# GpSimd holds back its work on the last pair until VectorE's joint chain of moments is through

## The reference

```python
for i in range(4):
    q, k, v = x @ Wq[i] + bq[i], x @ Wk[i] + bk[i], x @ Wv[i] + bv[i]
    Q, K = elu(q) + 1, elu(k) + 1
    KV, Ksum = sum over tokens of K * v, sum over tokens of K
    V = Q * KV / (Q * Ksum + 1e-6)
    x = ln(gelu(gelu(V @ Wo[i] + bo[i])) + x, ln1_s[i], ln1_b[i])
    x = ln(gelu(gelu(x @ W1[i] + b1[i]) @ W2[i] + b2[i]) + x, ln2_s[i], ln2_b[i])
x = layernorm(x_in + x)
h = layernorm(gelu(x @ ternary(W_fc).T), ln_w, ln_b)
x = layernorm(x + h @ ternary(W_proj).T)
```

## Time and profile before

| | |
|---|---|
| median of 3 runs | 479.62 us (478.72 to 481.2) |
| the profiled execution | 478.65 us, span 476.5 us |
| PE busy | 442.0 us (93%) |
| DVE busy | 402.6 us (85%) |
| ACT busy | 371.9 us (78%) |
| POOL busy | 13.9 us (3%) |
| DMA | 10.40 MB, mean 22 GB/s |

### The profile page before, as it was taken

The page is one execution under the profiler, slowest core; times in us unless marked ns, Lnnn a source line. Parts: engine busy times, 40 slices in busy tenths (PEclk is TensorE's granted clock), DMA queues, the critical chain, the costliest instruction groups (busy, mean ns, idle before and its releaser), DMA issues.

```text
span 476.5 us, 6527 instructions
## 1 busy us (share of the span) xinstructions
PE 442.0 (93%) x2074; PEld 309.2 (65%) x2074; DVE 402.6 (85%) x1391; ACT 371.9 (78%) x483; POOL 13.9 (3%) x19
## 2 busy tenths in 40 slices
PE   7697999999999999999999999999989999799992
PEld 6465665756575656566656665667566756688992
DVE  5988889995989698969896988698878897978897
ACT  3989877989897989798889888989888717778106
POOL 0000000000000000000000000000000003230000
PEclk9978999999999999999999999999999999999997
DMA  8200000000100000001000000000010102000003
GB/s 285 70 2 0 22 3 0 1 0 1 45 0 2 23 0 1 1 0 45 0 2 1 1 0 1 0 1 2 0 45 12 34 7 82 2 0 23 2 23 132
DMA packets 5360, 10.40 MB, mean 22 GB/s; under 512 B 848, under 2 KB 1872, under 8 KB 5328
## 3 DMA queue, kind: packets, MB, share of 16 engines
q1 hardware_dynamic: 5040, 9.47, 6.1%
q10 hardware_dynamic: 288, 0.52, 0.3%
HBM read 7.90 MB, written 2.10 MB: 21 GB/s over the span
## 4 chain that ended last, share of the span: by engine, by line
PE 41%; DVE 32%; ACT 19%; issue 7%; DMA 1%; ACTq 0%; SPq 0%; DVEq 0%
PE tile L1249 10%; PE tile L1268 7%; PE tile L1226 6%; PE tile L1222 6%; PE tile L1223 5%; DVE stats L770 5%; ACT y L369 3%; DVE y L911 3%; DVE nt L777 2%; ACT y L374 2%; PE tile L1339 2%; PE tile L1328 2%; ACT aa L388 2%; DVE y L880 2%; ACT kq L348 2%
## 5 line engine op out<-in xcount | busy, mean ns | idle before, releaser
L1249 PE MATMUL tile<-h,w 128*128 128x512 f32 x256 | 113.9, 595 | 0.9 <-ACT h L395 0.7
L1222 PE MATMUL tile<-xh,wh 128*128 128x512 f32 x224 | 97.6, 436 | 6.1 <-DVE xh L793 3.4
L1223 PE MATMUL tile<-xh,wl 128*128 128x512 f32 x224 | 89.2, 398 | 0.0
L1249 PEld LDWEIGHTS tile<-h,w 128*128 128x128 f32 x256 | 47.4, 190 | 54.8 <-issue 51.7
L395 ACT ACTIVATE h<-tile,vec 128x1024 f32<-128x1024 f32 x64 | 71.0, 1117 | 13.1 <-PE tile L1226 12.3
L1226 PE MATMUL tile<-xl,wh 128*128 128x512 f32 x224 | 71.1, 398 | 0.7 <-DVE xl L298 0.3
L403 ACT ACTIVATE nt<-tile,work 128x128 f32<-128x128 f32 x140 | 50.7, 482 | 11.3 <-DVE work L739 11.3
L1222 PEld LDWEIGHTS tile<-xh,wh 128*128 128x128 f32 x224 | 42.6, 190 | 24.9 <-DVE xh L793 5.3
L770 DVE BATCH_NORM_STATS2 stats<-tile 128x6 f32<-128x128 f32 x256 | 52.8, 280 | 0.1
L1226 PEld LDWEIGHTS tile<-xl,wh 128*128 128x128 f32 x224 | 41.6, 188 | 13.5 <-DVE xl L799 2.7
L1223 PEld LDWEIGHTS tile<-xh,wl 128*128 128x128 f32 x224 | 42.8, 191 | 9.1 <-issue 2.2
(11 more groups left out here) (173 smaller groups left out, 669.6 us busy)
## 6 DMA issues: line engine op xcount, KB each, us to landing
x<-x_t SPq DMA_DIRECT2D x7, 512.0 KB, 4.1
out_r<-x SPq DMA_DIRECT2D x8, 256.0 KB, 2.0
raw_u<-layers SPq DMA_DIRECT2D x4, 256.0 KB, 3.2
w<-layers SPq DMA_DIRECT2D x4, 256.0 KB, 3.3
raw_a<-layers SPq DMA_DIRECT2D x4, 192.0 KB, 2.8
x<-x_t ACTq DMA_DIRECT2D x2, 256.0 KB, 3.9
wo<-layers SPq DMA_DIRECT2D x4, 64.0 KB, 4.2
fc<-fc_t SPq DMA_DIRECT2D x1, 256.0 KB, 6.5
```

Of the source, the lines that this page charges most:

```text
L1222: pe.matmul(dst, wh[:, w0:w0 + P], xh[:, part(n, p, at)], start=True, stop=False)
L1223: pe.matmul(dst, wl[:, w0:w0 + P], xh[:, part(n, p, at)], start=False, stop=False)
L1249: mm = pe.matmul(dst, w2[:, (t - 1) // 2 % 2, j * P:(j + 1) * P], h[:, p, j * PAIR + at:j * PAIR + at + BANK], start=(j == 0), stop=(j == ...
```

## The change

It does three things. GpSimd gets two waits ahead of `shifted(pool, 3)`, on both halves of the tail's joint chain. `moments` and `rsqrt_of` are written anew as one helper to each level, and `moments` calls them level by level. The wait with which `moments` ended for the "g" norm (of the hidden layer) has moved into `final_sum`, which waits on `moment["g"]` or `moment["x"]` itself; six of its first instructions so carry one semaphore more. Wrappers with new names (`first_input`, `vectors`, `input_high`, `warm_up` and the like) hold the same calls in the same order.

```diff
@@ gpsimd
             shifted(pool, 1)
             with_constant(pool, 1)
             shifted(pool, 2)
+            for q in range(2):
+                pool.wait_ge(moment["2"][q], MOMENT_STEPS * STEPS)
             shifted(pool, 3)
             with_constant(pool, 0)
             with_constant(pool, 2)
@@ vector
-            def moments(*norms):
...
-                rsqrt_of([(w[0], w[1] + 2, w[2], float(width_of[n[0]]) ** 0.5) for n, w in work_of.items()])
-                for n in norms:
-                    done, base, (rstd, shift, m, v, a, b) = work_of[n]
-                    dve.wait_ge(done, base + 9)
-                    if n[0] != "g":
-                        dve.scalar_tensor_tensor(shift, m, -0.5, rstd, ALU.mult, ALU.mult).then_inc(done, 1)
+            def guess_squared(k, t, p):
+                done, base, (rstd, shift, m, v, a, b), width = chain(k, t, p)
+                dve.wait_ge(done, base + 3)
+                dve.tensor_tensor(a, b, b, ALU.mult).then_inc(done, 1)
...
+            def row_shift(k, t, p):
+                done, base, (rstd, shift, m, v, a, b), width = chain(k, t, p)
+                if k != "g":
+                    dve.wait_ge(done, base + 9)
+                    dve.scalar_tensor_tensor(shift, m, -0.5, rstd, ALU.mult, ALU.mult).then_inc(done, 1)
 
             def moments(*norms):
+                for level in (sums, mean_square, variance, guess, guess_squared, near_one, quadratics, first_product, root,
+                              row_shift):
+                    for n in norms:
+                        level(*n)
...
             def final_sum(p, u):
                 n, q = p // 2, p % 2
                 dve.wait_ge(x_cb[p], 1)
+                if n == 0:
+                    dve.wait_ge(moment["g"][q], HIDDEN_STEPS)
+                else:
+                    dve.wait_ge(moment["x"][q], 3 * MOMENT_STEPS)
                 for z in range(HALF):
```

More of the change, by code:

```diff
@@ L674, in _, with chain @@
         def _(dve):
-            def norm_work(k, t, p, u=None):
-                pair, rows = home(k, t, p), slice(0, ROWS) if u is None else slice(u * HALF, (u + 1) * HALF)
+            def chain(k, t, p):
+                pair = home(k, t, p)
                 if k == "h":
[L680 to L683, removed]
@@ L741, in rsqrt_of @@
[L741 to L764, removed]
@@ new lines, in chain, with sums @@
+                    done, first, at = moment["x"][p], 2 * MOMENT_STEPS, "g"
+                else:
+                    done, first, at = moment[k][p], call_of(k, t) * (HIDDEN_STEPS if k == "g" else MOMENT_STEPS), k
+                return done, first + 3, [value(at, pair, z) for z in range(NCOLS)], {"g": 1, "h": FF}.get(k, P)
+            def sums(k, t, p):
+                done, base, (rstd, shift, m, v, a, b), width = chain(k, t, p)
+                at = home(k, t, p)
+                if k == "g":
+                    for u in range(2):
+                        means = tile[TAIL_SLOTS["p", at, u]][:, :].rearrange("p (b c) -> p b c", c=BANK)[:, :, P:2 * PW:PW]
+                        dve.wait_ge(p_mm[p], 2 * t + u + 1)
+                        dve.tensor_copy(m[:, u * HALF:(u + 1) * HALF].rearrange("p (b c) -> p b c", c=2), means).then_inc(
+                            done, 1)
+                    dve.wait_ge(squared[at], FT)
+                    dve.tensor_scalar(b, squares[:, at, :], 1.0 / FF, OUTER_EPS, ALU.mult, ALU.add).then_inc(done, 1)
+                    return
+                if k == "h":
+                    dve.wait_ge(squared[at], FT)
+                    even, odd, even2, odd2 = (stats_h[:, p, :, c] for c in (1, 4, 2, 5))
+                else:
+                    dve.wait_ge(stats_ready[k][p], call_of(k, t) + 1)
+                    even, odd, even2, odd2 = (stats[k][:, at, :, c] for c in (1, 4, 2, 5))
+                dve.tensor_tensor(a, even, odd, ALU.subtract).then_inc(done, 1)
+                dve.tensor_tensor(b, even2, odd2, ALU.add).then_inc(done, 1)
+                dve.tensor_tensor(m, even, odd, ALU.add).then_inc(done, 1)
@@ new lines, in mean_square, with variance @@
+            def mean_square(k, t, p):
+                done, base, (rstd, shift, m, v, a, b), width = chain(k, t, p)
+                if k == "g":
+                    dve.wait_ge(done, base)
+                    dve.scalar_tensor_tensor(a, m, -1.0, m, ALU.mult, ALU.mult).then_inc(done, 1)
+                else:
+                    dve.wait_ge(done, base - 2)
+                    dve.scalar_tensor_tensor(a, a, width / 4.0, a, ALU.mult, ALU.mult).then_inc(done, 1)
+            def variance(k, t, p):
+                done, base, (rstd, shift, m, v, a, b), width = chain(k, t, p)
+                dve.wait_ge(done, base + 1)
+                if k == "g":
+                    dve.tensor_tensor(v, a, b, ALU.add).then_inc(done, 1)
+                else:
+                    dve.scalar_tensor_tensor(v, b, width * (BLOCK_EPS if k in "12" else OUTER_EPS), a, ALU.add,
+                                             ALU.add).then_inc(done, 1)
@@ new lines, in guess @@
+            def guess(k, t, p):
+                done, base, (rstd, shift, m, v, a, b), width = chain(k, t, p)
+                dve.wait_ge(done, base + 2)
+                dve.tensor_scalar(b.bitcast(I32), v.bitcast(I32), -0.5, GUESS, ALU.mult, ALU.add).then_inc(done, 1)
+            def guess_squared(k, t, p):
+                done, base, (rstd, shift, m, v, a, b), width = chain(k, t, p)
+                dve.wait_ge(done, base + 3)
+                dve.tensor_tensor(a, b, b, ALU.mult).then_inc(done, 1)
@@ new lines, in near_one, with quadratics @@
+            def near_one(k, t, p):
+                done, base, (rstd, shift, m, v, a, b), width = chain(k, t, p)
+                dve.wait_ge(done, base + 4)
+                dve.scalar_tensor_tensor(a, a, (LEAD * width ** 0.5) ** 0.25, v, ALU.mult, ALU.mult).then_inc(done, 1)
+            def quadratics(k, t, p):
+                done, base, (rstd, shift, m, v, a, b), width = chain(k, t, p)
+                lead = (LEAD * width ** 0.5) ** 0.25
+                dve.wait_ge(done, base + 5)
+                dve.scalar_tensor_tensor(v, a, Q1 * lead, a, ALU.add, ALU.mult).then_inc(done, 1)
+                dve.scalar_tensor_tensor(shift, a, Q2 * lead, a, ALU.add, ALU.mult).then_inc(done, 1)
@@ new lines, in first_product, with root @@
+            def first_product(k, t, p):
+                done, base, (rstd, shift, m, v, a, b), width = chain(k, t, p)
+                dve.wait_ge(done, base + 6)
+                dve.scalar_tensor_tensor(b, v, C1 * (LEAD * width ** 0.5) ** 0.5, b, ALU.add, ALU.mult).then_inc(done, 1)
+            def root(k, t, p):
+                done, base, (rstd, shift, m, v, a, b), width = chain(k, t, p)
+                dve.wait_ge(done, base + 8)
+                dve.scalar_tensor_tensor(rstd, shift, C2 * (LEAD * width ** 0.5) ** 0.5, b, ALU.add, ALU.mult).then_inc(done, 1)
@@ L1344, in projected, with warm_up @@
                     mm.then_inc(p_mm[p % 2], 1)
-            pe.wait_ge(const_ready, 7)
-            for _ in range(WARM_UP):
-                pe.matmul(tile[3][:, 0:P], ones[:, :], ones[:, :], start=True, stop=True)
+            def warm_up():
+                pe.wait_ge(const_ready, 7)
+                for _ in range(WARM_UP):
+                    pe.matmul(tile[3][:, 0:P], ones[:, :], ones[:, :], start=True, stop=True)
+            warm_up()
             attention_in("k", 0, 0)
```

78 lines of the change are left out of this document (23 added, 55 removed).

## The result

The changed kernel takes 475.28 us in the median of 6 executions (474.29 to 476.38), the kernel before 479.09 in the median of 6 (478.58 to 481.2). The ratio is 0.9918, with a 95% interval from 0.9904 to 0.9933. The profiled execution takes 475.41 us with a span of 473.5, 3.0 us less than the span before. Its time fell by 3.24 us, from 478.65: 0.24 us of that lies outside the span, in what an execution takes beyond its first to last instruction.

What follows compares the result with a forecast made beforehand. No engine bounds throughout; the last chain changes hands, and GpSimd stalls VectorE's joint chain by 3.01 us. Of this 2.63 arrives, other edits cost 0: 479.62 - 2.6 = 477.0 us, range 475.9 to 479.3.

Steps and rivals of the forecast that it cites:

- The stall and its size: Joint chain on VectorE: two levels, L751 and L754, stand while GpSimd works, 0.83 and 2.18 too long, 3.01 us together.
- How much arrives: From the joint chain to the outer norm's statistics: 2.63 of the 3.01 us arrives and stays whole to the end.
- Both receivers that I let decide: At pair 3's rows: TensorE's matmuls until 407.80 and ScalarE's `hidden_gelu` until 406.56 limit how much earlier work can start.
- The short wait of TensorE for ScalarE's rows: At pair 3's rows: a TensorE idle time of 0.1 replaces the present one.
- No stall elsewhere: VectorE's twelve rows of L777, read from PSUM beside GpSimd's shift and constant, still take 3.9 us; upper bound 3.5 us.
- the rival that moves the stall there: The stall moves to `rows`, eleven of which stand until 409.15: 0.2 to 0.3 us slower, 479.9; chance 0.05.
- their cover: GpSimd's last two constants end 1.0 us before the hidden layer's chain needs both inputs in SBUF; that margin stays.
- The waits of `final_sum`: Six first instructions of the last sums wait for one semaphore more: taken as 0, upper bound 0.4 us.
- the edits that were priced at nothing: Helpers and wrappers leave the instruction order on VectorE, ScalarE, TensorE and SyncE unchanged and cost nothing; `final_sum` waits taken as 0.
- the sum: Whole kernel: profiled 478.65 - 2.63 = 476.0; the same difference on the median, 479.62 - 2.6 = 477.0, 0.54% less.
- theory A: From the experiments: time at 1.2 GHz near the start has nothing to do with the edit; ratio back to 0.993 to 0.9945.
- D: Theory from the experiments: the edit changes how long TensorE runs at 1.2 GHz near the start; ratio 0.991 to 0.992.

Runs made afterwards that it cites:

- The waits alone: Kernel before plus only the two GpSimd waits ahead of pair 3's shift: 476.23 us against 478.89, ratio 0.9928; again 475.59 against 479.17, ratio 0.9926.
- the helpers alone: Changed kernel without the two GpSimd waits (helpers, wrappers, moved waits stay): 478.94 us against 478.89, ratio 0.9998; again 479.2, ratio 1.0001.
- the kernel with two memsets: Changed kernel plus two 128x2560 GpSimd memsets in a row from the landing of pair 3's input: 478.25 us in a single execution.
- the longer hold: Kernel before plus a third GpSimd instruction, a 128x1024 sum between pair 3's shift and pair 0's constant: 481.39 us against 479.17, ratio 1.0045.

## Why the prediction was right, and where it was wrong

- **The stall and its size: right.** Each level beside GpSimd takes 0.25 once it is alone; the joint chain ends at 405.1 with 3.0 less in it. The waits alone take the stall away, the helpers alone leave it.
- **How much arrives: right.** 2.63 was worked out, 2.70 measured between the two marks. Both receivers that I let decide, ScalarE in its `hidden_gelu` and TensorE in its last matmuls, are where they were put, and the statistics wait for TensorE (0.45 us) and not for VectorE's own list, as worked out. The short wait of TensorE for ScalarE's rows (0.1) did not come.
- **No stall elsewhere: right.** Twelve rows took 3.92 beside a shift and a constant; the rival that moves the stall there falls. The constants ended at 424.66, 1.04 us ahead of the first instruction of the hidden layer's chain with both inputs in SBUF, so their cover stayed.
- **The waits of `final_sum`: mis-sized.** Taken as 0, they measured 0.1 us in the traces: 61.61 to 61.65 us behind the second mark in four profiles of the change, 61.42 to 61.56 in seven of the kernel before, 61.45 and 61.57 with the waits on GpSimd alone, and 61.60 and 61.65 with the helpers and moved waits alone. (A span is given to 0.1 us, so each has 0.05 of play.) The chain that ended last shows where, at the first sum of pair 1, which in the kernel before begins right behind the hidden layer's chain. Before, and then the change:

```profile
455.10 0.18 DVE work_g L764
455.28 0.02 issue
455.30 2.16 DVE y L949 x8
```
```profile
452.00 0.18 DVE work_g L765
452.18 0.03 issue
452.21 0.02 DVEq L957
452.23 0.06 issue
452.29 0.16 DVE y L966
452.45 0.10 issue
452.55 1.89 DVE y L966 x7
```

The eight sums end 2.18 us behind the chain before and 2.26 behind it in the change. On the other side, the edits that were priced at nothing also take 0.23 us off what lies outside the span, which the prediction did not consider. Its reading of the earlier trace rows, that a fulfilled wait shows nothing, did not carry over to this place.
- **The step that failed is the sum**: "The same difference on the median gives 479.62 - 2.6 = 477.0." It took the difference within one profiled execution for that of all, and so put at nothing, without a reason, whatever the stall costs in the executions that were not profiled. Measured were 479.09 and 475.28, 3.8 us apart. Of the 1.7 us between the forecast of 477.0 and 475.28, 0.5 is the base, a median of three executions that six put lower, and 1.2 is the difference. I had seen TensorE's 2.16 us of idle time and had priced it at its length alone. In part of the executions the kernel before pays for it a second time, 1.28 us through the lower clock, and no profile of the change shows that part. By the executions at 0.981 or less, the kernel before loses 479.00 - 478.65 = 0.35 us in the mean by it. It is a rough estimate: the mean clock does not tell a loss at 410 us from one more at the start (the kernel with two memsets read 0.981 with 13.7 us at the start and none at 410; the second profile of the helpers alone read 0.983 with 6.8 and 3.4), so the share may be larger or smaller. This term explains a part of the miss and not all of it.
- **What like with like gives.** TensorE runs at 1.2 GHz for 3.4, 6.8, 10.2 or 13.7 us in all between 21 and 46 us, in any kernel. Profiles with 10.2 and no loss behind the stall: 478.51 us in the mean of five of before, 475.68 of three of the change, 2.83 apart. The stretch (2.7), the waits of `final_sum` (-0.15) and the time outside the span (0.24) add up to 2.8. So between comparable executions nothing is missing.
- **What stays open.** All 24 executions of the change have a mean of 475.38, the 89 of before 479.00 (the six beside the first result have no clock on record; with them it is 479.02): 3.6 us. Less 2.8 and about 0.35 for the clock behind the stall, some 0.45 are left. An execution with less time at 1.2 GHz near the start tends to be faster: `second_sum(8, 1)` came at 396.63 and 397.28 in two profiles with 3.4, at 397.18 to 398.80 in four with 6.8, at 397.92 to 399.33 in thirteen with 10.2 and at 399.34 in the one with 13.7. So the rest would be that the change met shorter losses at the start more often. Its instructions up to 398 us are before's, which speaks for chance, but twelve executions more did not bring it back (0.993 and 0.9919), and neither theory A nor D can be called shown. That the measured time fell below the range and not just inside its lower end rests on this open part as much as on the failed step.

## What to carry to other kernels

A small instruction in a dependent chain that takes many times its usual length, and moves on within 0.1 us of the end of a GpSimd instruction, was held by it here each time; its wait shows as busy time. Put GpSimd's work beside VectorE instructions that read PSUM, with a semaphore that the chain has anyway: two waits took away all of the 2.7 us. And price idle time of TensorE at more than its length, in a sum over executions: whether the clock survives a gap is something that one profile does not tell. For differences of half a per cent, compare profiles that lost the same time to the clock elsewhere.

## What the runs showed of the hardware

- TensorE's granted clock fell to 1.2 GHz for 3.4 us after idle gaps of 2.14 and 2.18 us in two of nine profiles with the unlengthened stall, and stayed at 2.4 GHz in the other seven, with gaps of 2.10 to 2.22; it fell after one of 3.79 us in the profile of the longer hold. It did in none of four profiles of the change, where the gap is gone.
- GpSimd holds VectorE by operands: a shift or a sum (which read SBUF) held levels of one and of two SBUF inputs, a memset held one of one input for 2.0 us and spared those of two. None held an instruction with a PSUM source: twelve rows took 3.92 us beside a shift and a constant, and with the end of a memset beside the first of them.
- GpSimd's sum of 128x1024 took 1.90 us with one tensor as both inputs and 2.35 to 2.40 with `cb` broadcast as the second.
